# Side work of the neighbourhood stage drained two units after its fill and without fillers beside it; the first trial units of the global stage in two pairs of PSUM banks

## What is computed

```python
# 1: neighbourhood attention (7x7 window, 4 heads of 16) and an MLP
x = x + proj(softmax(q . k_window + bias) @ v_window)      # on layernorm(x)
x = x + gelu(layernorm(x) @ fc1 + b1) @ fc2 + b2
# 2: global attention, 8 heads of 64 over the 1024 tokens of an image
t = tokens(x)
t = t + softmax(q k^T) v Wu + bu                           # on layernorm(t)
# 3: 33 routed steps of attention and/or feed-forward, chosen by argmax of the first token
t = t + routed(layernorm(t))
```

## Time and profile before

| | us |
|---|---|
| median of 3 runs | 647.61 (645.7 to 652.51) |
| profiled execution | 652.3 |
| its span, first to last instruction | 650.5 |
| PE busy in the span | 574.0 (88%) |
| DVE busy | 402.9 (62%) |
| ACT busy | 316.0 (49%) |
| mean granted clock of PE | 0.929 |

### The profile page before, as it was taken

The page is one execution under the profiler, slowest core; times in us unless marked ns, Lnnn a source line. Parts: engine busy times, 40 slices in busy tenths (PEclk is TensorE's granted clock), DMA queues, the critical chain, the costliest instruction groups (busy, mean ns, idle before and its releaser), DMA issues.

```text
span 650.5 us, 8966 instructions
## 1 busy us (share of the span) xinstructions
PE 574.0 (88%) x3311; PEld 241.9 (37%) x3312; DVE 402.9 (62%) x730; ACT 316.0 (49%) x460; POOL 50.7 (8%) x105
## 2 busy tenths in 40 slices
PE   6999998997499999999999999999999825599962
PEld 5554554554123234233333333233323211267611
DVE  5655546365775665867866776666552264798642
ACT  3645354834145584555555545555455323466330
POOL 6031133130110000100000010000000010000000
PEclk9999798968689999999999999999999958799976
DMA  4000000000000000000000000000000000000001
GB/s 107 1 2 2 1 2 1 1 2 1 1 0 1 0 1 1 2 0 2 0 1 1 0 2 1 1 8 0 1 1 0 1 4 2 13 1 2 1 0 33
DMA packets 9507, 3.22 MB, mean 5 GB/s; under 512 B 8820, under 2 KB 9079, under 8 KB 9463
## 3 DMA queue, kind: packets, MB, share of 16 engines
q1 hardware_dynamic: 8182, 2.61, 1.8%
q10 hardware_dynamic: 1281, 0.01, 0.1%
HBM read 2.09 MB, written 0.52 MB: 4 GB/s over the span
## 4 chain that ended last, share of the span: by engine, by line
PE 61%; issue 26%; DVE 8%; ACT 2%; POOL 1%; SPq 0%; DVEq 0%; POOLq 0%; DMA 0%; ACTq 0%
PE PS L779 11%; PE PS L756 10%; PE PS L741 4%; PE PS L666 4%; PE PS L680 4%; PE PS L693 3%; DVE most L1542 2%; PE PS L517 2%; PE PS L707 2%; PE PS L489 2%; PE PS L501 2%; PE PS L990 2%; PE PS L724 2%; PE PS L794 2%; PE PS L563 2%
## 5 line engine op out<-in xcount | busy, mean ns | idle before, releaser
L1542 DVE TENSOR_REDUCE most<-PS 128x2 f32<-128x1024 f32 x128 | 156.4, 1222 | 77.3 <-PE PS L741 77.0
L1191 ACT ACTIVATE PT<-PS 128x1024 f32<-128x1024 f32 x128 | 130.9, 1024 | 111.2 <-PE PS L756 110.6
L779 PE MATMUL PS<-PT,V 128*64 128x512 f32 x512 | 137.6, 617 | 0.0
L756 PE MATMUL PS<-qS,aS 128*128 128x512 f16 x512 | 133.1, 383 | 0.0
L756 PEld LDWEIGHTS PS<-qS,aS 128*128 128x128 f16 x512 | 44.9, 98 | 77.4 <-ACT PT L1191 21.1
L741 PE MATMUL PS<-aS,qS 64*128 64x512 f16 x128 | 51.0, 398 | 11.3 <-DVE most L1542 10.6
L1147 ACT ACTIVATE prob<-sbias,negm 128x320 f32<-128x320 f32 (+1 forms) x64 | 34.3, 537 | 45.4 <-DVE negm L1588 45.2
L741 PE MATMUL PS<-aH,qS 64*128 64x512 f16 x128 | 51.0, 398 | 0.0
L666 PE MATMUL PS<-ident 128*128 128x256 f16 x128 | 40.9, 320 | 7.3 <-DVE negm L1588 6.4
L1311 POOL TENSOR_TENSOR rstd<-var,minus_half 128x8 f32<-128x8 f32 x8 | 13.2, 1645 | 379.4 <-DVE var L1417 379.4
L336 DVE COPY PT<-PS 128x384 f32<-128x384 f32 (+1 forms) x32 | 16.7, 523 | 33.7 <-PE PS L693 33.7
(11 more groups left out here) (194 smaller groups left out, 709.0 us busy)
## 6 DMA issues: line engine op xcount, KB each, us to landing
xall<-in_x_dram SPq DMA_DIRECT2D x2, 256.0 KB, 4.4
out_dram<-x SPq DMA_DIRECT2D x4, 128.0 KB, 2.1
w<-in_L_attn_Wq_dram SPq DMA_DIRECT2D x2, 128.0 KB, 2.5
w<-in_L_attn_Wk_dram SPq DMA_DIRECT2D x2, 128.0 KB, 2.6
w<-in_L_attn_Wv_dram SPq DMA_DIRECT2D x2, 128.0 KB, 2.6
fc<-in_L_conv_fc_w_dram SPq DMA_DIRECT2D x2, 64.0 KB, 2.6
wu<-in_L_attn_Wu_dram SPq DMA_DIRECT2D x2, 64.0 KB, 2.4
w1s<-in_L_ffn_ffn_w_dram SPq DMA_DIRECT2D x2, 64.0 KB, 2.1
```

Of the source, the lines that this page charges most:

```text
L756: mm = pe.matmul(PS[:, score_banks(t) + lane, :], aS[:, k0:k0 + P], qS[:, part, lane, toks], start=(part == 0), stop=(part == 1))
L779: mm = pe.matmul(PS[cols, 6 + g % 2, :], V[:, img * NT + kt, cols], PT[:, g % 2, lane, kt, :], start=(kt == 0), stop=(kt == NT - 1))
L1191: act.activation(PT[:, g % 2, :, phase, :], PS[:, b0:b0 + 2, :], ACT.Exp).then_inc(c1["exped"], 1)
L1542: dve.tensor_reduce(most[:, g % 2, u // 2, u % 2, :], PS[:, 2:4, :], AX.X, ALU.max, negate=True)\
```

## The change

1. Every drain step in `at_step` moves one step later, so side work is drained two units after its fill (`mlp`: 51 and 52 filled, 54 drained; `a` moves whole from 59/60 to 60/62).
2. No filler stands before the scores and turns of a step that fills side work (`BUSY_STEPS`, 16 steps), nor from `TRY_STEP` on.
3. `PIECE_STEPS` has two entries, (62, 64) and (65, 67). The third pair of pieces (4 and 5) is projected in t = 0 and t = 1 of the global stage.
4. `TRY_STEP` is 65 and `STEP0` -7: 4 trials in the neighbourhood loop instead of 6, the others follow in t = -7 on. Trials 1, 3, 5, 7 use banks 4 and 5, and trials 2 to 8 wait only for the maximum of the trial two before.
5. `turn_shift(0)` waits for 4 pieces instead of 6; the moments for image 1 begin at t = -1 instead of -2.

```diff
-        at_step = {("x", 1): (9, 10), ("q", 1): (12, 13), ("k", 1): (15, 16), ("v", 1): (19, 20),
-                   ("wT", 0): (24, 25), ("wk", 0): (27, 28), ("mix", 0): (30, 31), ("wu", 0): (33, 34),
-                   ("y", 0): (45, 46), ("h", 0): (47, 48), ("H", 0): (49, 50), ("mlp", 0): (51, 53),
-                   ("a", 0): (59, 60)}
-        PIECE_STEPS = ((61, 62), (64, 65), (66, 67))
-        TRY_STEP, STEP0 = 63, -5
+        at_step = {("x", 1): (9, 11), ("q", 1): (12, 14), ("k", 1): (15, 17), ("v", 1): (19, 21),
+                   ("wT", 0): (24, 26), ("wk", 0): (27, 29), ("mix", 0): (30, 32), ("wu", 0): (33, 35),
+                   ("y", 0): (45, 47), ("h", 0): (47, 49), ("H", 0): (49, 51), ("mlp", 0): (51, 54),
+                   ("a", 0): (60, 62)}
+        PIECE_STEPS = ((62, 64), (65, 67))
+        TRY_STEP, STEP0 = 65, -7
+        BUSY_STEPS = {at for at, _ in at_step.values()} | {at for at, _ in PIECE_STEPS} | {at_step["mlp", 0][0] + 1}
+        def trial_bank(a):
+            return 4 if 1 <= a <= 7 and a % 2 else 2
-        MOMENT_T, DIVIDE_T, TURN_T, HIDDEN_T, GELU_T = -2, 5, 7, (9, 15, 16, 17), 18
+        MOMENT_T, DIVIDE_T, TURN_T, HIDDEN_T, GELU_T = -1, 5, 7, (9, 15, 16, 17), 18
@@ nat_score(u)
-                keep_busy(PS[:, u % 2, :])
+                if u - 2 not in BUSY_STEPS and u - 2 < TRY_STEP:
+                    keep_busy(PS[:, u % 2, :])
@@ nat_turn(u)
-                keep_busy(bank)
+                if u + 1 not in BUSY_STEPS and u + 1 < TRY_STEP:
+                    keep_busy(bank)
@@ try_scores(a)
-                if a:
-                    pe.wait_ge(c1["tried_max"], a)
+                if a >= 2:
+                    pe.wait_ge(c1["tried_max"], a - 1 if a <= 8 else a)
-                    mm = pe.matmul(PS[:, 2 + lane, :], qS[rows, 0, lane, q0:q0 + P], keys[rows, k0:k0 + BLK],
+                    mm = pe.matmul(PS[:, trial_bank(a) + lane, :], qS[rows, 0, lane, q0:q0 + P], keys[rows, k0:k0 + BLK],
@@ turn_shift(g)
-                pe.wait_ge(piece_drained, min(2 * (g + 3), 2 * NG))
+                pe.wait_ge(piece_drained, min(2 * (g + 3), 2 * NG) if g else 4)
@@ global loop, PE
+                if t in (0, 1):
+                    pe.wait_ge(piece_drained, 4 + t)
+                    project(4 + t, small_bank(0))
@@ global loop, ACT
+                if t in (0, 1):
+                    high_query(4 + t, small_bank(0))
@@ global loop, DVE
+                if t in (1, 2):
+                    low_query(3 + t, small_bank(0))
```

## The result

| | before | after |
|---|---|---|
| median, us | 650.06 (645.7 to 653.25, 4 runs) | 663.65 (661.79 to 670.9, 4 runs) |
| ratio to before, 95% interval | | 1.0234 (1.0128 to 1.0341) |
| profiled execution, us | 652.3 | 670.9 |
| its span | 650.5 | 669.1 |
| mean granted clock | 0.929 | 0.895 |

The kernel became slower by 2.3%, 13.6 us; 648.0 was predicted, in a range up to 656.

A forecast was written before the change was run, and what follows sets the result against it. The prediction took PE, with its clock, to bound the neighbourhood stage. Its terms, -3.8 + 3.9 + 1.5 + 2.8 - 5.0 + 0.9 = +0.3, on 647.6 us gave 648.0 us, no change that can be told; range 640 to 656.

The forecast's parts named there:

- What bounds the kernel: Neighbourhood stage: PE bounds it, waits are a twentieth of it, and PE's own time depends on the granted clock.
- Drains two units behind: Side drains up to the last MLP fill: new waits 6.6 us, old ones 2.7 in the same steps; +3.9 us.
- The clock around the MLP: At the MLP: the clock falls two steps earlier, second fill and step 52 at the lower level; +1.5 us.
- rival 1: Steps 18 to 33: the clock falls earlier and stays down; +9.8 us, 657.7 us; chance 0.15.
- Fillers: Neighbourhood stage: 14 fillers before scores and 15 before turns dropped; -3.8 us.
- From the last MLP fill to the first piece: Stretch between these two points: 25.1 us instead of 22.4, nearly all at the lower clock before; +2.8 us.
- rival 2: After the MLP: the clock holds, first piece 18.7 us after the last MLP fill; 640.0 us; chance 0.17.
- Trials in two pairs: Tail, first piece to first scores: DVE works without a pause, 20 us against 25.1; -5.0 us.
- Pieces 4 and 5 in t = 0 and 1: Start of the global stage: two projections on PE, which is the bound there; +0.9 us, bounds 0 and +1.8.
- Rival 3: Neighbourhood stage: queues hold more ahead, so the 6.6 us of new waits fall away; 641.3 us; chance 0.13.

The follow-up runs named there:

- e9: The whole changed kernel with trains of 256-column matmuls put into its waits and before the first pieces; 643.56 us.
- e12: The changed kernel with the drains of k, wk and H put back to one step after the fill; 646.88 us.
- e5: The kernel before with only the drain of k one step later (17 instead of 16); 655.68 us.
- e8: The kernel before with the new tail, its old drains, and trains of matmuls in the waits it already had; 639.99 us.
- e11: The kernel before with the new tail, old drains, trains of matmuls in its old waits, and fillers beside side work dropped; 636.69 us.
- e2: The kernel before with only the fillers dropped in steps that fill side work; 646.91 us.
- e4: The kernel before with the new tail alone, drains and fillers as before; 642.64 us.
- e1: The changed kernel with all 128 fillers back, lag of two and new tail kept; 660.91 us.
- e3: The kernel before with the drains of x to H one step later, all fillers and the old tail kept; 661.51 us.
- e6: The kernel before with only the drain of H one step later (51 instead of 50); 656.76 us.
- e7: The kernel before with the drains of x to H one step later and trains of 256-column matmuls in the waits; 648.31 us.
- e10: The kernel before with new tail, old drains, trains in its old waits, and 18 more matmuls before the first values; 640.65 us.

## Why the prediction was wrong, by its steps

*What bounds the kernel: right.* PE and its clock.

*Drains two units behind: right in place and size.* New waits of 0.85, 1.7, 1.05, 1.0, 0.2 and 1.8 us were laid out from program order, 6.6 together; measured 0.85, 1.46, 0.24, 1.10, 0.30 and 2.13, 6.1. That of v is short in a stretch at the lower clock; in e9 and e12, where the clock is up at this place, it is 1.06.

*The clock around the MLP, +1.5 us: the step that failed.* It priced one earlier fall, at one place, within a bound of 2.5. The new waits behind k and wk stood in the sum with their own length only, and the clock behind them with nothing. In the profiled execution of the changed kernel the low stretches of the stage grew by 36.2 us (67.3 against 31.1); at 0.42 that is 15.2 us. Up to the last MLP fill +1.6 was predicted, of which 0.1 without the clock; measured 149.22 against 132.46, +16.8. By the rows these are:

- behind k and wk, 23.0 low us more than at 66.5 and 107.4 before: 9.7 us;
- at the MLP, low from 140.00 to 149.22, through both fills: 3.9 us;
- at the beginning of the stage, where all matmuls have the durations of the lower level at first, a rise that came late: 2.0 us. It is not shown to belong to the change; e12, the same program up to step 15, was up by 45.6 us.

Together 15.6; the rest, 1.2 us, is not laid out. For the last item, PE before (first two rows) and after. The filler takes 0.29 us at 42.66 before and still 0.39 at 46.83 after, and the same matmuls of `nat_values` start 2.0 us later:

```profile
42.66 0.29 PE L666 MATMUL PS<-ident 128*128 128x256 f16 x1
45.69 1.00 PE L707 MATMUL PS<-PT 128*32 128x128 f32 x24
...
46.83 0.39 PE L671 MATMUL PS<-ident 128*128 128x256 f16 x1
...
47.67 1.00 PE L714 MATMUL PS<-PT 128*32 128x128 f32 x24
```

The mechanism stood in rival 1, with 9.8 us and a chance of 0.15. The rule of the Trainium skill beside it ("TensorE: Matmul & The Clock Gate", "A second HAM failure mode: psum-queue depth-cycling") is that short pauses between groups of matmuls make the clock swing between its levels. The traces bear it out in part: the clock fell behind the one added wait of 1.46 us in e5, but behind the wait of 1.54 us in only four of nine executions (last section). The evidence for a higher chance was in the rows: of the waits of before up to the MLP the only one above 1 us, 1.54, was followed by a fall, and I predicted two waits longer than that (1.7 and 1.8) and then argued from one of 0.94 that had done no harm. Two more rows spoke for it. The fall at 134.8, put down to the MLP's 64-column matmuls, comes 0.3 us behind a wait of 0.89; and the longest wait behind a side drain is not 0.94 but 1.09, behind a:

```profile
134.54 0.28 PE L666 MATMUL PS<-ident 128*128 128x256 f16 x1 [0.89 <-DVE negm L1588]
...
153.97 0.28 PE L666 MATMUL PS<-ident 128*128 128x256 f16 x1 [1.09 <-DVE negm L1588]
```

Rival 1 was off in its place too: the clock didn't stay low from step 18 to 33, it fell behind k, came back at wT, and fell again behind wk. That its 9.8 us come near the 9.7 above is luck.

*Fillers, -3.8 us: right where the clock holds* (e8 against e11, 100.0 against 96.2 us for the same work), and worthless where it doesn't (the profiled execution of e2).

*From the last MLP fill to the first piece: right in the sum.* 25.1 us predicted at the lower clock; 149.22 to 174.89 is 25.7. In e8, where the clock holds and a stands one step earlier, the same way takes 16.6 us (128.45 to 145.03), so rival 2 was right as a mechanism and not what happened.

*Trials in two pairs, -5.0: too large.* From 25.1 before, the tail came down to 22.8 us, not 20, in the changed kernel (-2.3) and to 21.2 in e4 (-3.9). The maxima ran at 1.13 us as predicted:

```profile
187.38 0.60 PE L748 MATMUL PS<-aS,qS 64*128 64x512 f16 x1 [1.94 <-DVE most L1554]
...
188.51 0.61 PE L748 MATMUL PS<-aS,qS 64*128 64x512 f16 x1 [0.53 <-DVE most L1554]
```

What was late was the beginning: trial 0 at 181.57, 6.7 us after the first piece in place of 4.4. PE was at the lower clock there, and the second pair of pieces waited 0.87 us for the first to be drained (179.77).

*Pieces 4 and 5 in t = 0 and 1, +0.9:* from the first scores to those of t = 3 there are 8.3 us (197.67 to 205.95) against 6.8 before (179.89 to 186.71), +1.5, within the bound of 1.8.

*Rival 3, the lag takes the waits away: fell.* Of the 6.6 us of new waits that it was to remove 6.1 are there.

## What to carry to other kernels

Moving a drain later on an in-order engine doesn't only add slack: look at what else stands in the step it moves to, and whether that waits for the same producer; a drain that filled idle time may end up in a row with work that is due. Where PE's clock falls behind its waits, as it did here, price a wait of PE by the slow stretch that follows it, not by its own length: here 0.8 us of wait was followed by 5 us of loss. Whether a given wait is followed by a fall changed from run to run, so such a price wants a chance beside it. And a wait that can't be removed can be made harmless by matmuls whose result nobody reads, into a bank that is free anyway.

## What the runs showed of the hardware that was not expected

Idle time well below 2 us can be enough for a fall, and is not always. In the profiled executions, the longer waits of PE ahead of the pieces that found the clock up, by whether the granted clock fell in the wait or within 2.6 us behind it:

| wait | us | a fall | no fall |
|---|---|---|---|
| behind k, lag of two | 1.45 to 1.46 | after, e1, e3, e5 | |
| before the MLP's second layer, lag of two | 1.84 to 2.13 | after, e1, e3, e6 | |
| behind a layernorm's moments, step 42 | 1.54 | before, e2, e4, e12 | after, e1, e3, e5, e6 |
| behind the MLP's drain | 0.89 to 1.14 | before, e5, e9, e12 | e2, e4, e7 |
| behind wk, lag of two | 1.10 | after | e1, e3 |
| behind v, lag of two | 1.06 | e9 | e12 |
| behind wT | 0.93 to 0.94 | | before, e4, e6 |
| behind q | 0.79 to 0.85 | e2 | before, after, e1, e3, e4, e5, e6, e12 |

So the length of the single wait does not decide alone, and what else does is open. Nor does every fall have such a wait ahead: in before, e6 and e7 the clock falls at v (66.4 to 67.2 us) with no wait above 0.22 us in the 5 us ahead. Behind k the clock then stayed low for about 20 us in which PE was busy nearly all the time (19.65 of 19.65 us in e5).

Nor did a train of matmuls raise the clock at the beginning of the stage in the profiled execution of e10. The 18 full-array matmuls, back to back, changed nothing: the units behind them have the durations of the lower level, as PE's timeline shows. The other eleven executions of e10 have a lower mean granted clock (0.931 to 0.941 against 0.952), though nine of them took less time; what the clock did at their beginning is not known.

```profile
20.54 4.05 PE L663 MATMUL PS<-ident 128*128 128x256 f16 x18
24.38 4.16 PE L577 MATMUL PS<-wqkv,PT 65*128 65x64 f32 x20
...
29.33 0.55 PE L699 MATMUL PS<-k0S,q0S 32*128 32x224 f16 x2
```

Each of the 18 takes 0.21 us, and a unit's score of 224 columns 0.55 us, where it takes 0.36 at the upper level (93.96 in the changed kernel); that lasts until 50 us. The granted clock of these first stretches is given as 1.00 all the same:

```profile
30.00:49.00 19.00, 19.00 (x84) 8.87 (x84) 10.21 (x36) 7.20 (x16) 4.60 (x11) 1.00 0.00 0
```

So for the first 40 to 50 us the durations, and not the granted clock, tell the level. What ends this first low stretch is open; in all kernels it ended near the transposes of the second image's norm, between 41 and 50 us.
